# Zeros by ScalarE, selectors first, half-group loads and a new hand-written order in an attention and mixture-of-experts kernel

## The reference

```python
# x: (16, 256, 256) = 4096 tokens of 256;  ctx the same shape
def attention(q, k, v):            # 16 heads of 16 numbers; the "sequence" is the list of heads
    scores = einsum('bsqd,bskd->bsqk', qh, kh) / sqrt(16)     # 16 x 16 for each token
    attn = softmax(where(tril, scores, -1e18))
    return einsum('bsqk,bskd->bsqd', attn, vh)

def ffn(x):
    logits = x @ gate_w.T + gate_b                 # 8 experts
    top1 = argmax(logits)
    out = sum over e of where(top1 == e, relu(x @ w1[e].T + b1[e]) @ w2[e].T + b2[e], 0)
    return out                                     # 256 -> 1024 -> 256

x = x + attention(layernorm(x), ctx, ctx)
x = x + ffn(layernorm(x))
```

## Time and profile before

| | |
|---|---|
| median of 3 runs | 486.3 us (484.06 to 491.79) |
| the profiled execution | 486.96 us, of which 485.2 us lie between the first and the last instruction |
| PE busy | 397.5 us (82%) |
| PEld busy | 337.0 us (69%) |
| DVE busy | 348.3 us (72%) |
| ACT busy | 179.6 us (37%) |
| POOL busy | 206.3 us (43%) |
| mean granted TensorE clock | 0.904 |

### The profile page before, as it was taken

How to read it: one execution, slowest core, us unless ns; L and a number is a source line. 1 busy time by engine, 2 the same in 40 slices (tenths; PEclk the granted TensorE clock), 3 DMA queues, 4 the chain that set the end, 5 groups by cost and what they waited for, 6 DMA issues and landing times.

```text
span 485.2 us, 16314 instructions
## 1 busy us (share of the span) xinstructions
PE 397.5 (82%) x5967; PEld 337.0 (69%) x5967; DVE 348.3 (72%) x777; ACT 179.6 (37%) x317; POOL 206.3 (43%) x213
## 2 busy tenths in 40 slices
PE   0134868896887967987859999999999999999992
PEld 0024767796787866977847887777788878887871
DVE  7987879689965965777547886787666667666662
ACT  3333255552633332332323433334334333333420
POOL 8336375234574456623711342465332233232221
PEclk9999999999999755565559999999999999999998
DMA  8999668899786665676621423465333222222300
GB/s 287 415 296 237 139 149 238 213 269 261 172 212 141 157 134 125 161 162 124 218 61 33 79 83 123 132 192 179 70 71 76 77 64 64 70 63 67 85 24 0
DMA packets 105162, 69.39 MB, mean 143 GB/s; under 512 B 78077, under 2 KB 88190, under 8 KB 104576
## 3 DMA queue, kind: packets, MB, share of 16 engines
q1 hardware_dynamic: 75696, 56.67, 43.9%
q10 hardware_dynamic: 25984, 3.21, 4.8%
q0 software_dynamic: 3408, 8.46, 4.7%
HBM read 48.28 MB, written 12.57 MB: 125 GB/s over the span
## 4 chain that ended last, share of the span: by engine, by line
PE 58%; DMA 10%; POOL 7%; SPq 7%; issue 7%; DVE 6%; ACT 2%; ACTq 1%; POOLq 0%; DVEq 0%
PE s_ps L1216 22%; PE at_ps L1231 7%; DMA arena<-qv_hl 7%; PE pv_ps L1231 7%; SPq L298 7%; PE pv_ps L1130 5%; PE at_ps L1232 4%; PE pv_ps L1232 3%; PE s_ps L1098 3%; POOL sorted_rows L1037 2%; PE tr_ps L1143 2%; PE st_ps L1183 2%; DMA arena<-x 2%; POOL qv_hl L990 1%; PE lg_ps L1158 1%
## 5 line engine op out<-in xcount | busy, mean ns | idle before, releaser
L1216 PEld LDWEIGHTS s_ps<-arena 128*128 x1872 | 131.5, 99 | 44.3 <-issue 5.8
L1216 PE MATMUL s_ps<-arena 128*128 128x128 f16 x1872 | 156.8, 221 | 2.4 <-issue 2.3
L903 DVE SCALAR_TENSOR_TENSOR arena<-arena,s_ps 128x512 f32<-128x512 f32 x78 | 53.6, 687 | 43.6 <-PE s_ps L1216 43.5
L1063 POOL DMA_INDIRECT result<-arena x39 | 38.8, 995 | 79.1 <-DVE arena L927 76.6
L1098 PEld LDWEIGHTS s_ps<-k_hl,arena 128*128 128x128 f16 x1536 | 53.9, 118 | 26.1 <-DMA arena<-qv_hl 21.7
L1098 PE MATMUL s_ps<-k_hl,arena 128*128 128x16 f16 x1536 | 54.1, 181 | 19.6 <-DMA arena<-qv_hl 19.0
L1130 PE MATMUL pv_ps<-a_hl,arena 128*128 128x16 f16 x1536 | 53.9, 181 | 18.2 <-DMA arena<-qv_hl 14.0
L1130 PEld LDWEIGHTS pv_ps<-a_hl,arena 128*128 128x128 f16 x1536 | 52.7, 118 | 21.5 <-DMA arena<-qv_hl 19.0
L1056 POOL TENSOR_TENSOR arena<-arena 128x256 f32<-128x256 f32 x39 | 29.8, 764 | 75.5 <-DMA arena<-b 68.7
L1231 PE MATMUL at_ps<-arena,k_in 128*128 x160 | 60.3, 379 | 0.8 <-DVE k_hl L913 0.6
L1231 PE MATMUL pv_ps<-arena,x_in 128*128 x152 | 57.6, 379 | 0.2
(11 more groups left out here) (139 smaller groups left out, 616.4 us busy)
## 6 DMA issues: line engine op xcount, KB each, us to landing
arena<-w SPq DMA_DIRECT2D x28, 512.0 KB, 6.1
arena<-sorted_rows SPq DMA_DIRECT2D x39, 130.0 KB, 2.7
arena<-b SPq DMA_DIRECT2D x39, 128.0 KB, 3.7
arena<-qv_hl SPq DMA_DIRECT2D x70, 64.0 KB, 3.9
k_in<-k_t SPq DMA_DIRECT2D x16, 256.0 KB, 3.9
v_in<-v_t SPq DMA_DIRECT2D x16, 256.0 KB
arena<-x SPq DMA_DIRECT2D x4, 1024.0 KB, 12.2
o_sb<-x_r SPq DMA_DIRECT2D x16, 256.0 KB, 3.5
```

Source lines behind the costliest of these rows:

```text
L903: eng.scalar_tensor_tensor(out=h_in[:, c].rearrange("p (k t) -> p k t", t=P), in0=bias, scalar=W_SCALE, in1=h_ps[c][:].rearrange("p (k t) ...
L1063: eng.indirect_dma_start(out=out, out_offset=bass.IndirectOffsetOnAxis(ap=rows[:, r, :].bitcast(I32)[:, D + 2:D + 3], axis=0), in_=rows[:, ...
L1216: k = eng.matmul(o, weights_of(j, w + k_ * H + n * P, P), xt[:, j % 2, k_ * P:(k_ + 1) * P], start=k_ == 0 and w is HI_1 and xt is xt_hi, ...
```

## The change

Five things are changed.

1. The zeros of two of the three diagonal operands were written by GpSimd (two MEMSETs of 128 x 4096). Now ScalarE writes them, by four copies of a zero column (`rowmax[:, 0:1]`, which GpSimd sets to zero first) into 128 x 2048 halves. The semaphore `s_zero`, for which the spreads wait, so counts to 4.
2. DVE first zeroed the third operand (`q_flat`) and then made the small selectors (`turn_of`, `unit_of`, `owner`, `sel`). Now the selectors come first, then the zeros, and then at once the two operands of the gate (`gate_sum`, `gate_bd`).
3. The rows of x for the statistics are loaded as eight half groups (512 KB each, a semaphore each), not four groups (1 MB each).
4. Two lanes of GpSimd (`tables`, `row_tails`) are due earlier.
5. All tables of due numbers are replaced, and with them the order on every engine. `tile_at(0)`, the due number of the stream's start, goes from 252.9 to 237.0.

```diff
-        s_xs = [sem(f"s_xs{n}") for n in range(NG)]
+        s_xs = [[sem(f"s_xs{g}_{n}") for n in range(2)] for g in range(NG)]
...
         def tile_at(j):
-            return 252.9 + TILE * j
+            return 237.0 + TILE * j
...
             def load_stats():
                 for g in range(NG):
-                    yield (-1.1, 6.6, -17.1, 15.6)[g]
-                    eng.dma_start(staged[:, g], x_v[g]).then_inc(s_xs[g], 16)
+                    for n in range(2):
+                        yield (5.0, 5.0, 12.9, 9.2, -3.4, 1.6, 16.3, 10.8)[2 * g + n]
+                        part = slice(n * G // 2, (n + 1) * G // 2)
+                        eng.dma_start(staged[:, g, part], x_v[g][:, part]).then_inc(s_xs[g][n], 16)
...
             def spread():
                 for i in range(NC):
-                    yield (40.4, 54.8, 64.0, 76.9, 96.8, 105.5, 119.1, 128.2, 140.9, 155.5, 165.1, 181.1, 195.3,
-                           208.2, 220.0, 225.7)[i]
-                    sp.wait_ge(s_zero, 2)
+                    yield (37.7, 50.6, 63.7, 77.9, 90.1, 97.4, 112.9, 124.9, 139.9, 146.8, 163.4, 175.5, 191.7,
+                           202.8, 213.8, 225.8)[i]
+                    sp.wait_ge(s_zero, 4)
...
+            def zeros():
+                for d in range(2):
+                    for n in range(2):
+                        yield (-2.9, -11.7, 3.2, 0.1)[2 * d + n]
+                        act.wait_ge(s_nil, 1)
+                        half = (of_expert(E - 1), v_flat)[d].bitcast(F32)[:, n * SLOT // 4:(n + 1) * SLOT // 4]
+                        eng.copy(half, rowmax[:, 0:1].to_broadcast([P, SLOT // 4])).then_inc(s_zero, 1)
...
                 eng.memset(eighths, 0.125).then_inc(s_eighths, 1)
-                eng.memset(of_expert(E - 1).bitcast(F32), 0.0).then_inc(s_zero, 1)
-                eng.memset(v_flat.bitcast(F32), 0.0).then_inc(s_zero, 1)
```

287 lines of the change are left out of this document (144 added, 143 removed), and 12 rows, old and new, of tables (act, half, op1).

## The result

The changed kernel takes **496.8 us** (median of 4 runs, 493.82 to 498.11) against 487.7 (4 runs, 484.06 to 491.79) of the kernel before on the same chip: ratio 1.0183, interval 1.0139 to 1.0227. Run again it took 496.7, ratio 1.0194 (1.0149 to 1.0239). The forecast of 478.0 was wrong, and so was its range (471 to 488): the change makes the kernel 1.8% slower, just inside the 2% that the prediction called no difference, with an interval that leaves no change out.

A forecast was written before the change was run, and what follows sets the result against it. Attention was taken as bound by its loop of spread, landing and PV, the stream by a full PE. 486.96 - 4.3 (transition) - 4.0 (start) = 478.7 us, 0.7 less for the median: 478.0, range 471 to 488.

The forecast's parts named there:

- How much of the start reaches the last PV?: Attention loop: of the earlier start, between 0 and -8 us was to reach the last PV; -4 us taken.
- The slack: Attention loop: 15 turns at 12.45 us against a shortest of 10.2, some 2.2 us per turn of other waits.
- First queries, scores and spread: Start: statistics near 8.0 us, first queries at 19.1, about 4.6 earlier; scores(0) near 29.5, scores(1) near 33 instead of 40.71.
- the same chain: Start, statistics to first queries: 12.1 us as before, less three BN_STATS at 0.35, so queries at 19.1.
- Zeros, selectors, half loads: Start: four ScalarE copies near 2.06 us each, no long DVE copy for `sel`, half loads costed at nothing.
- The transition: Last PV to first ups: ups at 240.3, 11.8 us earlier; 6.9 us moved into the stream, 0.6 of wait there.
- The term of -4.3: Transition and stream: -11.8 + 6.9 + 0.6 = -4.3 us, bounds -7 to +1.
- The slower one: Attention: weights converted 6 us later, loads bunch, spreads queue behind them, PV waits for landings, +9 us: 491.0; chance 0.12.
- The other three: Whole start gain passes on, 474.0 (0.27); start lost in the loop, 482.0 (0.18); transition gives nothing, 482.3 (0.10).

The follow-up runs named there:

- a1: Changed kernel with ScalarE's late weight behind the second queries, and SP's load of chunk 2's x and chunk 1's first-query spread earlier: 491.0 us, ratio 1.0051.
- f1: c1 with the order of the kernel before for every step due between 121 and 191, the middle of the attention: 486.1 us, ratio 0.9968.
- p1: Kernel before, its order tables kept, with zeros on ScalarE, selectors first and half loads alone: 489.99 us, ratio 1.0035.
- c1: a1 with chunk 2's queries earlier on DVE, ScalarE and GpSimd, chunk 1's on DVE, and chunk 0's spread on SP: 490.56 us, ratio 1.0057.
- e1: p1 with the tables of b2, so all of the change but the attention's new order: 488.5 us, ratio 0.9985.
- b2: Kernel before with the new transition alone, and tile 0's low part ahead of group 2's plan on VectorE: 487.73 us, ratio 0.9971.
- a3: Changed kernel with the zeros of two diagonals written by GpSimd's two MEMSETs again: 495.23 us, ratio 1.0135.
- a2: Changed kernel with PV ahead of the scores of two chunks later on PE, for chunks 3, 8 and 10: 499.17 us, ratio 1.0224.
- a5: Changed kernel with the last eight heads of group 1's gates ahead of PV of chunk 8 on PE: 498.73 us, ratio 1.0262.
- c2: Changed kernel with group 1's last gates right behind PV of chunk 8, and SP's residual loads of chunks 8 and 9 earlier: 495.04 us, ratio 1.0173.
- d1: Changed kernel with ScalarE's exponential of chunk 9 ahead of its three DMAs of that chunk's spread: 494.26 us, ratio 1.0154.
- d3: d2 with PV of chunk 8 ahead of the scores of chunk 10: 490.74 us, ratio 1.0063.
- d2: Changed kernel with the edits of c1, c2 and d1, and SP's spread of chunk 3 ahead of a load of keys: 489.88 us, ratio 1.006.
- a4: Changed kernel with the rows for the statistics loaded by four transfers of 1 MB again: 494.39 us, ratio 1.0114.

## Why the prediction was wrong

**The step that failed** is the one headed "How much of the start reaches the last PV?". It put the ends at -8 and 0 and took -4; measured was +13.7 at the last spread, and the last PV came at 245.60, not near 227.8. It was wrong in its premise: it allowed the new order of the attention to pass a gain on or to absorb it, not to lose time of its own. The sentence that "the new tables reorder all of them" was written down and given no price. The runs put two losses in its place: the start, where mending the order around one weight gave back 1.3% of the time (a1), and the middle turns, 7.8 us, which the old order there gives back in full, while the turns behind it lose 2 to 3 again (f1). What the step asked has its answer in the runs too: of a first spread 2.6 us late nothing reached the last one (p1), of 5.4 us regained 3.7 did (c1 against the changed kernel). The slack that it reasoned with was misread as well: the shortest turn before was not 10.2 us but the last, 8.2 (215.82 to 224.06).

**First queries, scores and spread.** The statistics (9.22, forecast 8) and queries (21.36, forecast 19.1) were 1.2 and 2.3 us late and still ahead of before. The chain between them took 12.1 us, as before, not 11.1: DVE stands 0.85 us in it for the first weight's high part, ahead of the eighth statistic (12.46), and 1.08 us for the next group's rows (17.65). From there "the same chain" was not the same: scores(0) came at 32.03 instead of 29.5, scores(1) at 44.57 instead of 33. A weight stood ahead of the second queries in ScalarE's program; I costed ScalarE's DMAs there and not this wait. That alone does not make up the difference: without it scores(0) came at 33.86 and scores(1) at 39.31 (a1).

**Zeros, selectors, half loads.** Right in kind and nearly in size: 1.82 us a copy (2.06 forecast), 0.22 us for `sel`, statistics earlier (9.22; 11.11 in the old order of p1, 0.5 earlier). Together they are worth nothing in the end (p1, e1).

**The transition.** Right in its mechanism: no wait for `pay` ahead of the ups any more, and moved work paid in full, 6.8 us (6.9 + 0.6 forecast). From PV to the ups it takes 10.9 us, not 8.5. The gates start 5.5 us behind PV, not 4.2: DVE's steps of group 2's ranks stand ahead of its sum into `o_sb`, and the gates wait for one more of them behind it (`count_c`). So the ranks did not fit in the wait for `o_sb`, as I had it. And the ups need the low parts of *all* the weights (the program waits for the last of them), of which the last was begun at 254.48: in the changed kernel, in b2 and in f1 they start 1.3 to 1.5 us behind the end of that one. I had named late weights only through `xn2`. PV came 2.1 us later behind the spread, against 2.0 charged, but that is luck: I charged the issue of the weights, which was over (236.41) before the low part of the values, for which the spread waits, was ready (237.68). What ended PV's wait was the spread's landing, up to 5.1 us behind its issue (2.6 before). The term of -4.3 measured -2.5 (2.1 - 11.4 + 6.8).

**The rivals.** The slower one (491.0) was nearest in time, and its mechanism fell. Its place was to be PV's waits for landings; they did not grow. Waits from 36 to 238 us (against the earlier trace rows, which ends at 215):

```profile
PE pv_ps L1139 <- DMA arena<-qv_hl: 14.5, 6, 4.5
```

Nor do the zeros delay the weights (a3). What was near the truth in it is that weights and the attention meet on ScalarE: as a wait at the head of its queue for a load that landed late, not as spreads behind weights. The other three all took the start's gain as given and only asked how much of it is kept; none has a place for a loss in the loop.

**What stays open** is which steps of the middle's order hold its 8 us. Five edits in it (a2, a5, c2, d1 and d3's) shortened a turn and lengthened another, or did little; together they took at most 3.7 us from the middle (d2), and the old order as a whole mends it. Nor is it shown whether zeros on ScalarE or half loads cost something inside the new order (a3 and a4, with overlapping intervals).

## What to carry to other kernels

When a change replaces a whole table of orders, the order is the change: price it, with an end on the losing side, before the edits that can be named. Read the new order of each in-order engine for a wait with a late releaser ahead of an urgent step; here one weight conversion between two queries, with the loads that go with it, was worth 1.3%. Where mending single waits moves the loss from turn to turn, compare stretches over many variants, and put back the old order of one stretch as a whole.

## What the runs showed of the hardware

DVE's copy of 128 x 128 took 4.28 us beside GpSimd's MEMSET, and 0.22 us without; the three reductions just ahead of it, beside the MEMSET before that one, took 0.25 to 0.28. ScalarE's copy of 128 x 2048 took 1.82 us in a row of four.

A load of 512 KB issued at 14.57, while the DMA engines were busy throughout (1.03, 402 GB/s), landed 12.8 us later; the median of its group over the whole execution is 5.9.

The mean granted clock of TensorE was between 0.841 (p1, this execution 488.01 us) and 0.996 (c2, 493.99 us) in these profiles, 0.892 in the changed kernel (498.11), and the times do not follow it: in the attention, where it is at 0.50 for long stretches, a PV takes 3.37 us (at 245.60) as it did at the full clock before (3.35 at 69.87).
